# Fourth layer of a graph network: the head projection one tile later, the query product and the weighing steps on other slots, OT in two buffers

## What is computed

```
q, k, v = x @ Wq + bq, x @ Wk + bk, x @ Wv + bv      # 8 heads of 64
scores  = einsum('bmhd,bnhd->bhmn', q, k) / 8 + edge_bias[edges]
scores  = where(edges > 0, leaky_relu(scores, 0.2), -1e9)
out     = einsum('bhmn,bnhd->bmhd', softmax(scores), v).reshape(b, m, h * d) @ Wp + bp
x       = layernorm(x + out)
```

## Time and profile before

| | |
|---|---|
| median of 3 runs | 5223.71 us (5221.37 to 5227.72) |
| profiled execution | 5227.66 us, its span 5225.9 us |
| busy in the span | PE 4643.1 us (89%), DVE 4896.1 us (94%), ACT 4792.8 us (92%), POOL 3861.0 us (74%) |
| fourth layer | from about 3734 us to the end |
| its tiles 2 to 62 | 1387.0 us, a mean of 22.74 us a tile |

### The profile page before, as it was taken

One profiled execution on the slowest core, in us unless ns is written; L12 is line 12 of the kernel. 1 busy time (PEld: TensorE's weight loads), 2 busy tenths in 40 slices (PEclk: granted clock), 3 DMA queues, 4 the chain that ended last, 5 costly groups with the idle time before them and its releaser, 6 DMA issues. The chain is left out here.

```text
span 5225.9 us, 118915 instructions
## 1 busy us (share of the span) xinstructions
PE 4643.1 (89%) x48920; PEld 1850.1 (35%) x48920; DVE 4896.1 (94%) x5715; ACT 4792.8 (92%) x5793; POOL 3861.0 (74%) x3578
## 2 busy tenths in 40 slices
PE   7888888888888999989999999988799999999998
PEld 2222222222222223223232232334454554454554
DVE  7999999999999999999999999977699999999998
ACT  7999999999999999999999999969688888888887
POOL 8999999999999999999999999964122222222323
PEclk9999999999999999999999999989799999999999
DMA  1000000000000000000000000016211011101100
GB/s 44 21 21 21 21 17 21 21 21 21 17 22 21 21 21 21 21 17 21 21 21 21 17 21 21 21 32 189 72 35 32 28 36 32 35 28 36 32 28 16
DMA packets 144927, 155.32 MB, mean 30 GB/s; under 512 B 52294, under 2 KB 119622, under 8 KB 144390
## 3 DMA queue, kind: packets, MB, share of 16 engines
q1 hardware_dynamic: 143686, 147.65, 9.5%
q10 hardware_dynamic: 704, 0.07, 0.0%
HBM read 137.20 MB, written 2.10 MB: 27 GB/s over the span
## 5 line engine op out<-in xcount | busy, mean ns | idle before, releaser
L189 POOL TENSOR_SCALAR a_hid_p<-a_BLOS,a_PHI,a_PLO 128x1024 f32<-128x1024 f32 x2688 | 3153.6, 1197 | 82.8 <-PE apsS L315 70.2
L439 DVE SCALAR_TENSOR_TENSOR a_hid_p<-apsB,a_THI,a_hid_p 128x1024 f32<-128x1024 f32 x2560 | 3078.4, 1279 | 15.9 <-POOL a_hid_p L189 14.0
L315 PE MATMUL apsS<-a_hid_p,a_sel_high 128*32 128x512 f32 x10752 | 2647.9, 599 | 190.2 <-ACT a_hid_a L354 120.8
L315 PE MATMUL apsS<-a_hid_a,a_sel_high 128*32 128x512 f32 x6144 | 1925.2, 599 | 48.8 <-ACT a_hid_a L354 26.8
L315 PE MATMUL apsS<-a_hid_a,a_sel_low 128*32 128x512 f32 x5632 | 1685.0, 598 | 95.9 <-DVE a_hid_p L439 52.1
L354 ACT ACTIVATE a_hid_a<-a_BHI,a_ALH 128x1024 f32<-128x1024 f32 x1536 | 1696.1, 1149 | 0.0
L354 ACT ACTIVATE a_hid_a<-a_BLO,a_ALH 128x1024 f32<-128x1024 f32 x1408 | 1573.6, 1148 | 0.0
L315 PEld LDWEIGHTS apsS<-a_hid_p,a_sel_high 128*32 128x32 f32 x10752 | 584.7, 109 | 962.9 <-issue 551.6
L749 PE MATMUL m3S<-xT,Q 64*128 64x512 f32 x2048 | 596.8, 657 | 133.8 <-ACT x_even L793 90.4
L315 PEld LDWEIGHTS apsS<-a_hid_a,a_sel_high 128*32 128x32 f32 x6144 | 419.6, 109 | 564.3 <-issue 300.7
L315 PEld LDWEIGHTS apsS<-a_hid_a,a_sel_low 128*32 128x32 f32 x5632 | 376.1, 109 | 638.5 <-DVE a_hid_p L439 333.2
(11 more groups left out here) (184 smaller groups left out, 4059.0 us busy)
## 6 DMA issues: line engine op xcount, KB each, us to landing
a_adj_in<-adj SPq DMA_DIRECT2D x128, 512.0 KB, 3.4
adj_in<-adj SPq DMA_DIRECT2D x128, 512.0 KB, 3.8
Xr<-x_odd SPq DMA_DIRECT2D x128, 64.0 KB, 2.4
out<-yn SPq DMA_DIRECT2D x64, 32.0 KB, 1.5
x_even<-x SPq DMA_DIRECT2D x1, 256.0 KB, 2.8
wqT<-L_wqT SPq DMA_DIRECT2D x1, 130.0 KB, 4.2
wkT<-L_wkT SPq DMA_DIRECT2D x1, 130.0 KB, 4.2
wvT<-L_wvT SPq DMA_DIRECT2D x1, 130.0 KB, 4.3
```

The costliest lines, as they stand in the source:

```text
L189: gp.tensor_scalar(hid_p[:, at % RING_P, :], BLOS[:, g % 2, :], PHI[:, g % 2, m:m + 1], PLO[:, g % 2, m:m + 1], ALU.min, ALU.max).then_inc ...
L315: last = pe.matmul(psS[32 * q:32 * q + 32, h * HALF:(h + 1) * HALF], sel[:, 28 - 4 * p:60 - 4 * p], unit, start=s == 0 and layer == 0, sto ...
L439: dve.scalar_tensor_tensor(out=hid_p[:, at % RING_P, :], in0=psB[:, :], scalar=THI[:, g % 2, m:m + 1], in1=hid_p[:, at % RING_P, :], op0=A ...
```

## The change

```
-        STEPS = {0: (0, 4), 1: (4, 7), 3: (7, 10), 4: (10, 13), 5: (13, 16)}
+        STEPS = {0: (0, 3), 1: (3, 6), 3: (6, 9), 4: (9, 11), 5: (11, 14), 6: (14, 16)}
...
-            if (r, gap) == (0, 1) and m + 1 < T:
+            if (r, gap) == (2, 1) and m + 1 < T:
                 return [("query", *divmod(m + 1, tiles))]
-            if (r, gap) == (2, 1) and 2 <= m < T + 2:
-                return [("project", *divmod(m - 2, tiles))]
+            if (r, gap) == (1, 0) and 3 <= m < T + 3:
+                return [("project", *divmod(m - 3, tiles))]
...
-                        last = pe.matmul(psA[:, h * C:(h + 1) * C], OT[:, h, :], w["Wvp"][:, h, :],
+                        last = pe.matmul(psA[:, h * C:(h + 1) * C], OT[:, m % 2, h, :], w["Wvp"][:, h, :],
...
             def copy_o(m):
                 act.wait_ge(weighed, m + 1)
-                if m >= 1:
-                    act.wait_ge(aux_made, done("project", *divmod(m - 1, tiles)))
-                act.activation(OT.rearrange("p h (a i) -> p a h i", i=32),
+                if m >= 2:
+                    act.wait_ge(aux_made, done("project", *divmod(m - 2, tiles)))
+                act.activation(OT[:, m % 2, :, :].rearrange("p h (a i) -> p a h i", i=32),
...
                 m, r = divmod(i, PAIRS)
-                if r == 0 and 3 <= m < T + 3:
+                if r == 3 and 3 <= m < T + 3:
                     deviations(m - 3)
```

More of the change, by code:

```diff
@@ L1026, in build @@
                        adj_in=adj_in3[:, :], mask=sg("mask3", [P, 2, n], BF16),
-                       OT=sg("OT", [P, HEADS, P])[:, :, :], prod=sg("prod", [P, HEADS * C])[:, :],
+                       OT=sg("OT", [P, 2, HEADS, P]), prod=sg("prod", [P, HEADS * C])[:, :],
                        part=sg("part", [P, HEADS * C])[:, :], y=sg("y3", [P, 2, C]), yn=sg("yn", [P, 2, C]),
```

## The result

The changed kernel takes **5247.02 us** (median of 5 runs, 5244.27 to 5248.91), the kernel before 5226.38 us (5 runs, 5221.37 to 5227.72): a ratio of 1.004, 95% interval 1.0028 to 1.0051. It is slower by 0.4%, where the forecast was 5240 us and slower by 0.3%. The profiled execution took 5244.93 us, its span is 5243.1 us, 17.2 us more than before's 5225.9.

What follows compares the result with a forecast made beforehand. DVE was taken to set the floor, 21.21 us a tile, with clock falls on top. 60 x (22.41 + 0.63) + 21.2 = 1403.6, less 1387.0 = +16.6, ends -0.3: +16 us, so 5240 us, range 5203 to 5262.

Steps and rivals of the forecast that it cites:

- The stall: DVE's first minimum of the next r0 waits for POOL's late mask, about 1.85 us a tile, 60 times.
- What DVE gets back: Minima no longer stretched by mask (0.85 us) and additions (0.30 us); L679 blocks r1's second minimum for about 0.5 us.
- The idle on PE: PE idles 2.4 to 2.9 us for DVE's last transpose ahead of its first weighing piece.
- What a fall costs: TensorE's clock falls in 2 of 3 tiles, each costing DVE 0.95 us, so 0.63 us per tile.
- The tile: DVE's floor of a tile becomes 22.41 us, against 21.21 before, also in tiles that prepare a graph.
- the signs: Expected in the profile after: tiles of 23.1 us at clock 0.93 beside 22.4 us at 1.00.
- 6.8 us before T: End of r3's last first-half minimum, counted from T, the end of the first minimum of r0.
- The ends: Last tile 1.9 us less, work behind it about 1.6 us more; together -0.3 us.
- DVE makes Q a round or more before the scores that need it.: Step on PE's new order: Q is ready a round or more ahead of its scores.
- 1 (the clock holds): Rival: mask late but clock holds, with falls in under one tile in five; 5202 us, chance 0.2.
- Rival 4: No stall because mask is made early after all; DVE's floor 21.4 us, 5142 us, chance 0.04.

Runs made afterwards that it cites:

- e4: The kernel before with one edit of the change alone, statistics of y at the end of r3 instead of r0: 5398.62 us, ratio 1.0327.
- e11: The changed kernel, mask left late, with the query product at gap 0 of r2 and three weighing steps in its old place: 5249.84 us, ratio 1.0035.
- e5: e2 with the query product one gap earlier, at gap 0 of r2, and weighing steps 3 to 6 in its old place: 5110.32 us, ratio 0.9782.
- e2: The changed kernel with POOL making the next tile's mask right behind the additions, ahead of vare, rstd and yn: 5160.83 us, ratio 0.987.
- e1: The changed kernel with the statistics of y at the end of r2 instead of r3: 5173.55 us, ratio 0.9897.
- e8: The changed kernel with the mask of each tile from 4 on written twice: 5343.85 us, ratio 1.0227.
- e7: e2 with DVE doing rden and prod ahead of the first transpose of r1 instead of behind it: 5097.77 us, ratio 0.9757.

## Why the prediction was right

The mechanism was the predicted one, and so were most of its sizes:

- **The stall.** Predicted 60 x 1.85 us = 110 us. Measured 91.5 us in 57 waits; the whole ones are 1.82 us. Ahead of the first minimum of a tile where DVE has just copied for the next graph it is 1.22 us: the copy falls into the stall, as the prediction says, though its 110 us didn't take it off. In three tiles ACT's leaky relu came last.
- **What DVE gets back.** Mask never takes over 1.05 us, no minimum 2.05 us: as predicted. L679 costs 4512.25 - 4510.58 = 1.67 us to the successor where 1.14 is usual, 0.53 us against the predicted 0.50. The Trainium skill ("SBUF — State Buffer", on the two sides of SBUF) has an exclusive lock for the whole instruction, by which it would be L679's 0.73 us; the row is below that.
- **The idle on PE.** Predicted 2.4 to 2.9 us, measured 2.37 here and 2.7 at most; the mean of the 57 waits is 2.1, since it is shorter where a graph is prepared.
- **What a fall costs.** DVE waits 0.89 us for ACT behind it where 0.95 was predicted, with the slack at the place named. Falls come in 33 of tiles 3 to 62; predicted were 2 of 3, 40 of 60.
- **The tile.** 22.48 us at full clock, predicted 22.41; 23.2 to 23.5 fallen, where the signs said 23.1 and the sum's own 22.41 + 0.95 gives 23.36. Those that prepare a graph are no longer than others, as predicted. Tiles 2 to 62 became 14.2 us longer, predicted 16.6: the falls cost 10 us less than the forecast's 38, and the floor 4 us more, with 3 us for three long tiles (23.2, 23.8 and 23.8 us at full clock).

In the working for the idle, the printed terms of "6.8 us before T" have one 1.1 too many; 6.8 itself is right (6.9 in the trace after).

Wrong were three steps:

- **"The ends", -0.3 us.** They are +1.1. From the second minimum of r0 to the last transpose are 21.3 us, 1.1 less than before instead of 1.9; the last weighing is another 1.0 shorter (12.15 to 11.2 us up to the end of the copy to OT), which I had not counted; and the chain behind that copy went from 9.8 to 13.1 us, +3.3 instead of +1.6, since the last project also waits until DVE has read the one before it, and its additions wait on POOL for the normalising of tile 62.
- **The first two tiles** had no term. They are 5.2 us longer, at a granted clock of 0.65; before it was 0.82. It is PE's order: all eleven traces with the new one have 52.8 to 54.0 us here, and e4, with the old one and the late statistics, has 47.6 at 0.82. Which part of the order does it is open; no run varied these tiles alone.
- **"DVE makes Q a round or more before the scores that need it."** In the changed kernel PE waits for Q 36 times, up to 1.5 us. That cost nothing here (e11), because the mask was later still. Without the late mask it is the next limit: the earlier query is worth some 46 us (e5 against e2, 0.9782 against 0.987), about three quarters of it in the tiles around the preparation. The step's zero was right under its cover only.

The errors of the sum, -2.4 in the tiles, +1.4 in the tail, +5.2 at the start and -3.3 in layers that were not touched, nearly cancel; the exact hit of 17 against 16 us is luck in this part, the sign is not. Of the rivals, 1 (the clock holds) fails at its own condition of falls in under one tile in five; there were 33 in 60. Rival 4 (no stall, 5142 us) is what e1 looks like: its floor of 21.4 us is e1's regular tile, 21.37 us, and the 31 us up to 5173.55 are mostly the tiles around the preparation, 1.0 us longer each, which its sum took as regular. The change gave PE what it promised, 54 us, and lost 73 us on an order on POOL that it didn't touch.

## What to carry to other kernels

When a step is moved later, follow what stands behind its consumer in that consumer's queue: here the statistics moved, but it was the mask, in POOL's order behind the normalising, that became late, and one line on POOL (e2) turned +0.4% into -1.3%. A stall that opens an idle time on TensorE before its next piece can cost more than itself, here 1.4 us for each 1 us (e8), with the clock falling in more tiles the longer it is. Stretches of two kernels must be cut at the same instruction of the engine that bounds them: cut at the copy to OT, which had moved against DVE, neighbouring tiles of the changed kernel seem to take anything from 20.7 to 24.5 us, where DVE's own rhythm is 22.5 or 23.5. And a wait that costs nothing today should be written down with what covers it: Q's late place cost nothing beside the late mask and some 46 us without it.

## What was not expected of the hardware

- **A small operation on POOL can wait through two minima of DVE.** In e2 yn, a 128x64 operation, takes 2.65 us (shown there), and in e7 again; in the changed kernel, with DVE idle, 0.58 us. The minima that run beside it in e2 keep their usual durations:

```profile
4516.61 1.18 DVE L835 CUSTOM_DVE_ANT_0 Z<-Z,mask 128x1024 f32<-128x1024 f32 x1
...
4517.73 1.22 DVE L835 CUSTOM_DVE_ANT_0 Z<-Z,mask 128x1024 f32<-128x1024 f32 x1
```

  With L679 it was the other way round: there the minimum grew by 0.53 us, and L679 with it from 0.73 to 1.63 us. I can't say from these runs what decides which of the two waits. Yn's delay cost nothing that shows in e2, where the mask no longer stands behind it and DVE is hardly idle in regular tiles.
- **The clock at the layer's start.** With scores alone on PE and waits of 0.8 us for ACT between them, TensorE stays at 1.2 GHz for many groups on end (2.08 us each); in the kernel before, where a query product of 7 matmuls stood between two of the first groups, the second group after it took 1.13 us. The query product alone doesn't explain it: in the changed kernel one of the same size stands behind the sixth group (3759.82), and the next groups behind it still take 2.08 us (3764.23). And before, the clock fell again at 3764.52, after groups with idle times of 1.06 to 1.25 us. What decides it is open.
